# A two-layer graph network: layer 0 gathers x itself, its dense stage is woven into the end of the edge loop, and layer 1 gathers four quads ahead instead of eight

## The chip, the cores and the metric

The kernel runs on one core of one Trainium2 chip. The metric is the time of one execution on the device in microseconds (us), the median of several runs. TensorE (PE), VectorE (DVE), ScalarE (ACT), GpSimd (POOL) and SyncE (SP) each take their own instructions in order and wait for each other through semaphores.

## The reference

There are N = 6250 nodes with 128 features. 100000 drawn edges and one self loop for each node make E = 106250 edges, sorted by destination. Layer 0 is attention with one head, layer 1 one with eight heads, a learned edge term and an MLP behind it.

```
# layer 0
qk = x @ Wqk + bqk;  v = x @ Wv + bv
s[e] = clip(sum(qk[dst[e]] * qk[src[e]]) / sqrt(128), -5, 5)
attn = softmax of s over the edges of one dst
g = layer_norm(x + segment_sum(attn * v[src]) @ Wo + bo) * gamma + beta
x1 = layer_norm(x + g)
# layer 1
h = layer_norm(x1) * ln1_w
xl = h @ lin_l_w.T + lin_l_b;  xr = h @ lin_r_w.T + lin_r_b
z = leaky_relu(xl[src] + xr[dst] + edge_attr @ lin_edge_w.T, 0.2)
alpha = softmax over the edges of one dst of einsum("ehc,hc->eh", z, att)
x2 = x1 + segment_sum(xl[src] * alpha) + attn_bias
y = x2 + relu((layer_norm(x2) * ln2_w) @ fc_w.T) @ proj_w.T
out = layer_norm(x1 + y)
```

## The kernel before, in words

**Units.** The edges are cut into 832 tiles of 128 (`tiles`). Four tiles make a quad (`QT` = 4, 208 quads), four quads a group (`QUADS` = 4, 52 groups). The nodes are cut into 13 blocks of 512 (`node_groups`), each of four tiles of 128. Since edges are sorted by destination, the destinations of one tile lie in a window of 128 nodes that begins at its first one.

**Stages.** Six stages follow each other, each in a block of its own; all engines meet between two blocks. Node numbers are made ready (L110 to L143). The table `qkv_tab` is made: for each node one row of 1 KB in memory, half qk, half v (L160 to L210; PE L184, DVE L196, ACT stores at L204). Then come layer 0's edge stage (L214 to L378), its dense stage (L380 to L680), layer 1's edge stage (L683 to L1180) and the MLP (L1184 to L1490).

**Layer 0's edge stage.** For each quad, POOL issues four gathers (L260), each of which fetches the 128 rows of `qkv_tab` that belong to the sources of one tile. SP loads the four windows of destination rows (L249) and the row of edge positions `rel_bc` (L246). DVE makes from it the one-hot matrix `spread` (L334). PE multiplies it with the windows, which gives qk of each edge's destination, `q_dst` (L290), and transposes `spread` into `onehot_ps` (L296). DVE multiplies `rows` with `q_dst` and sums (`product`, L339), and clips (L375). ACT takes the exponential (L270) and scales the transposed one-hot matrix by it into `gather1` (L277). PE multiplies that with the v half of `rows` (L307) and with ones (L309) into `tile_sums`, which DVE adds to `node_sums` at the tile's first node (L348). `q_dst`, `spread` and `gather1` have two buffers each, `rows` four. The waits that tie POOL, SP and DVE to PE are these:

```
pool.wait_ge(summed, quad - QUADS + 1)            # POOL, ahead of the gathers of a quad
sp.wait_ge(q_spread, j * QUADS + q - QUADS + 1)   # SP, ahead of the windows of a quad
dve.wait_ge(summed, j * QUADS + q - 1)            # DVE, ahead of the adds of the quad two before
dve.wait_ge(q_spread, j * QUADS + q + 1)          # DVE, ahead of the scores
```

**The dense stage.** For each block of 512 nodes, PE transposes the sums of weights and spreads their inverses (L481, L490), DVE forms `mean_rows` (L561), PE multiplies by Wo (L500), DVE adds x with the bias (L569), and three layer norms follow (moments L536 and L539, roots on ACT L635, scaling on ACT L641 or DVE L589, POOL L618 to L626 for x, gamma and beta). PE transposes (L507) and multiplies with the weights of layer 1 (L516), DVE adds the biases (L582, L583), and ACT stores the tables `xl_tab` and `xr_tab`, rows of 512 bytes.

**Layer 1's edge stage.** It has the same shape: POOL gathers rows of `xl_tab` (L832), SP loads windows of `xr_tab`, edge attributes and edge positions (L812 to L816), PE makes z of a quad (L879, L883, L887; `z_ready`), ACT splits it (L843, L844), PE forms logits (L899), and once in four quads a chain of scans over DVE, PE and ACT makes the softmax. Nine quads after its z (`LAG` = 9) a quad's `message` is made on DVE (L974), multiplied on PE (L930) and added on DVE (L996). `rows` holds 16 quads (`ROWS`). POOL waits, ahead of the gathers of quad Q, for `message_made` of quad Q - 16 and for `z_ready` of quad Q - `AHEAD`, with `AHEAD` = 8.

## Time and profile before

| | us |
|---|---|
| median of 3 runs | 3092.32 (3090.11 to 3101.77) |
| profiled execution, its own time | 3122.75 |
| its span, first to last instruction | 3120.9 |
| mean granted TensorE clock in it | 0.862 of full speed |

Busy shares of the span: PE 71%, DVE 55%, ACT 21%, POOL 57%. No engine is busy all the time, so the waits say more than the shares. The profiled execution is 30.4 us (1.0%) longer than the median; sums made from its rows are made against 3122.75.

### The profile page before, as it was taken

How to read it: one execution, taken by the hardware profiler on the slowest of the kernel's cores; microseconds unless marked ns; L12 is line 12 of the kernel's file. 1: busy time of each engine (PE TensorE's matmuls, PEld its weight loads, DVE VectorE, ACT ScalarE, POOL GpSimd, SP SyncE). 2: the span in 40 equal slices, each digit the busy share in tenths (PEclk: the TensorE clock that was granted, in tenths of full speed). 3: DMA queues.
4: the chain of work that ended last, by engine and by line, in shares of the span. 5: the costliest groups of instructions: out<-in, count | busy, mean ns of one | idle time of the engine just before them, and what ended most of it. 6: DMA issues, size and time to landing. Idle time of an engine off the chain costs nothing. (4 is left out here: it accounts for less than half of the span.)

```text
span 3120.9 us, 55922 instructions
## 1 busy us (share of the span) xinstructions
PE 2211.6 (71%) x15187; PEld 1775.4 (57%) x15187; DVE 1709.5 (55%) x7262; ACT 652.8 (21%) x1876; POOL 1767.4 (57%) x1751
## 2 busy tenths in 40 slices
PE   4666666666666666656378777777777777788879
PEld 3666666666666666644255555555555555565656
DVE  4444444444444444478245555555655566565766
ACT  0222222222222222235021111111111111111123
POOL 2666666666666666644656555555555565555312
PEclk8988888888888888877688888888998999988869
DMA  6555555555555555513454444444444444444301
GB/s 212 158 150 148 152 151 150 149 151 151 149 149 151 151 151 149 139 44 88 141 163 130 121 137 133 123 130 138 137 134 120 132 139 137 137 124 130 92 15 38
DMA packets 392325, 413.24 MB, mean 132 GB/s; under 512 B 61167, under 2 KB 336367, under 8 KB 385360
## 3 DMA queue, kind: packets, MB, share of 16 engines
q1 hardware_dynamic: 304992, 233.79, 25.4%
q0 software_dynamic: 66560, 163.68, 19.3%
q10 hardware_dynamic: 20592, 13.63, 1.4%
q8 instruction: 79, 1.29, 0.2%
q14 instruction: 102, 0.84, 0.1%
HBM read 393.41 MB, written 17.47 MB: 132 GB/s over the span
## 5 line engine op out<-in xcount | busy, mean ns | idle before, releaser
L832 POOL DMA_INDIRECT rows<-xl_tab,src_cols x832 | 848.1, 1019 | 592.8 <-DVE message L974 356.4
L260 POOL DMA_INDIRECT rows<-qkv_tab,src_cols x832 | 819.7, 985 | 501.8 <-remote 250.1
L307 PE MATMUL tile_sums<-gather,rows 128*128 128x128 f32 x1664 | 401.6, 329 | 413.8 <-issue 396.8
L339 DVE CUSTOM_DVE_ANT_0 product<-rows,q_dst 128x128 f32<-128x128 f32 x832 | 233.7, 281 | 654.3 <-remote 641.5
L307 PEld LDWEIGHTS tile_sums<-gather,rows 128*128 128x128 f32 x1664 | 307.0, 230 | 460.7 <-issue 454.0
L996 DVE SCALAR_TENSOR_TENSOR node_sums<-node_sums,shrunk,tile_sums 128x128 f32 x832 | 280.7, 337 | 316.5 <-remote 294.6
L309 PE MATMUL tile_sums<-gather,ones 128*128 128x128 f32 x1664 | 380.8, 316 | 0.0
L883 PEld LDWEIGHTS z_ps<-spread,window 128*128 128x128 f32 x1664 | 253.3, 220 | 203.9 <-issue 101.8
L930 PE MATMUL tile_sums<-onehot,message 128*128 128x128 f32 x1664 | 304.3, 323 | 79.9 <-issue 72.0
L348 DVE TENSOR_TENSOR node_sums<-node_sums,tile_sums 128x256 f32 x832 | 350.8, 422 | 4.7 <-PE tile_sums L309 1.6
L930 PEld LDWEIGHTS tile_sums<-onehot,message 128*128 128x128 f32 x1664 | 245.3, 218 | 143.6 <-issue 129.9
L309 PEld LDWEIGHTS tile_sums<-gather,ones 128*128 128x128 f32 x1664 | 309.7, 232 | 0.3
L883 PE MATMUL z_ps<-spread,window 128*128 128x128 f32 x1664 | 261.7, 305 | 50.6 <-DVE spread L965 35.6
L899 PE MATMUL lg_ps<-z_act,att_pad 128*32 128x128 f32 x3328 | 206.7, 290 | 126.1 <-issue 125.1
L879 PE MATMUL z_ps<-attr,w_e 128*128 128x512 f32 x416 | 281.2, 764 | 7.6 <-issue 7.6
L290 PE MATMUL q_dst<-window,spread 128*128 128x128 f32 x1664 | 262.6, 310 | 20.8 <-issue 20.8
L290 PEld LDWEIGHTS q_dst<-window,spread 128*128 128x128 f32 x1664 | 246.0, 227 | 21.8 <-issue 21.6
L270 ACT ACTIVATE weight<-clipped 128x4 f32<-128x4 f32 x208 | 42.7, 205 | 981.7 <-DVE clipped L375 570.7
L277 ACT ACTIVATE gather<-onehot_ps,weight 128x128 f32<-128x128 f32 x832 | 237.7, 368 | 14.5 <-PE onehot_ps L296 2.8
L899 PEld LDWEIGHTS lg_ps<-z_act,att_pad 128*32 128x32 f32 x3328 | 106.1, 112 | 209.4 <-issue 205.0
L843 ACT ACTIVATE z_act<-z_ps 128x512 f32<-128x512 f32 x208 | 122.7, 590 | 425.8 <-PE z_ps L887 216.3
L984 DVE TENSOR_SCALAR onehot<-iota_row,rel_cols 128x128 f32<-128x128 f32 x832 | 179.6, 275 | 0.0
(153 smaller groups left out, 2532.8 us busy)
## 6 DMA issues: line engine op xcount, KB each, us to landing
window<-qkv_tab SPq DMA_DIRECT2D x832, 64.0 KB
attr<-in_attrT SPq DMA_DIRECT2D x52, 1024.0 KB
window<-xr_tab SPq DMA_DIRECT2D x832, 64.0 KB
rel_bc<-rel_rows SPq DMA_DIRECT2D x208, 128.0 KB
rel_bc<-rel_rows SPq DMA_DIRECT2D x52, 512.0 KB
rows<-qkv_tab,src_cols POOLq DMA_INDIRECT x832
rows<-xl_tab,src_cols POOLq DMA_INDIRECT x832
qkv_tab<-qkv ACTq DMA_DIRECT2D x13, 512.0 KB, 4.9
```

Source lines behind the costliest of these rows:

```text
L260: nc.gpsimd.indirect_dma_start(out=rows[:, q * QT + i, :], out_offset=None, in_=qkv_tab, in_offset=bass.IndirectOffsetOnAxis(ap=src_cols[: ...
L277: o = nc.scalar.mul(gather1[:, q % 2, i, :], onehot_ps[q % 2][:, i, :], weight[:, q % 2, i:i + 1])
L290: mm = nc.tensor.matmul(q_dst[q % 2][:, i, :], spread[:, q % 2, i * P:(i + 1) * P], window[:, q * QT + i, :], start=True, stop=True)
L307: nc.tensor.matmul(bank[:, i % 2, 0, :], rows[:, q * QT + i, P:], gather1[:, q % 2, i, :], start=True, stop=True)
L309: mm = nc.tensor.matmul(bank[:, i % 2, 1, :], ones[:], gather1[:, q % 2, i, :], start=True, stop=True)
L348: nc.vector.tensor_tensor(span, span, tile_sums[(q % 2) * 2 + i // 2][:, i % 2, :, :], ALU.add).then_inc(added, 1)
L832: nc.gpsimd.indirect_dma_start(out=rows[:, r, i, :], out_offset=None, in_=xl_tab, in_offset=bass.IndirectOffsetOnAxis(ap=src_cols[:, tile: ...
L879: nc.tensor.matmul(z[:], w_e[:], attr[:, s % 2, at:at + QW], start=True, stop=False)
L883: nc.tensor.matmul(z[:, i * P:(i + 1) * P], window[:, w, i, :], spread[:, Q % 2, i * P:(i + 1) * P], start=False, stop=False)
L899: mm = nc.tensor.matmul(lg_ps[s % 2][lanes, 0, :], att_pad[:, q, :], z_act[:, Q % 2, part, i * P:(i + 1) * P], start=(q == 0 and part == 0 ...
L930: mm = nc.tensor.matmul(tile_sums[Q % 2][:, i, :], message[:, Q % 2, i, :], onehot[:, Q % 2, i, :], start=True, stop=True)
L996: nc.vector.scalar_tensor_tensor(span, span, shrunk[:, Q // QUADS % 2, 1, tile % CHUNKS:tile % CHUNKS + 1], tile_sums[Q % 2][:, i, :], ALU ...
```

## The change

**One block for all of layer 0.** Stages one to four become one block without a meeting of the engines inside it, written out in full instead of in loops. Step T of it handles quad T's scores, the p of quad T + 1 and the sums of quad T - 1.

**x in place of qkv_tab.** POOL gathers rows of the input x, 512 bytes each, and waits only for the source numbers. The score is written as x[src] . p[dst] plus a constant of dst, where p = (x Wqk + bqk) Wqk^T, scaled. A table `p_tab` has 129 columns (516 bytes): p and the constant, from which the sum of the score starts. It is made in 13 blocks on PE by `make_p` (for each block four products with 129 columns and four with one row for the bias), kept and stored by ACT (`keep_p`): four blocks ahead of the first score, the other nine in steps 0 to 8. Wv and Wo are multiplied once into `w_vo` and applied to the sums.

**Halves and the one-hot matrix.** `p_dst` and `tile_sums` have one buffer for each half of a quad. PE does `spread_p` and `add_up` half by half. ACT makes the weighted one-hot matrix by itself (four Abs, an exponential, a negation, four Relu), so that the transposes of L296 go.

**The dense stage** starts at step `DENSE` = 204 and runs to step 222, one block of 512 nodes for a step, its parts 0 to 6 steps behind. Its weights are centred (`w_cen`), so that the tables need only a scale; biases go into the z of layer 1 (ACT) and the MLP; x1 is normalised in layer 1, on ACT, over quads 9 to 21. Tables have 50 tiles of 128 nodes instead of 52.

**Layer 1 and the MLP.** `AHEAD` goes from 8 to 4, `ROWS` stays 16. Semaphores of the scans are merged without a change of order. Two loads of a column and one of a bias row are added.

The core of the diff:

```diff
+    AHEAD0 = 4
+    SLOTS = 4
+    DENSE = 204
...
+                    if Q < node_groups:
+                        sp.wait_ge(p_stored[Q % 2], (Q // 2 + 1) * DMA)
+                    sp.dma_start(rel_bc[:, w, :], rel_rows[Q:Q + 1, :].to_broadcast([P, QW])).then_inc(window_in[w], DMA)
+                    for i, base in enumerate(window_bases(sp, s, Q % QUADS)):
+                        sp.dma_start(window[:, w, i, :], p_tab[bass.ds(base, P), :]).then_inc(window_in[w], DMA)
...
+                for Q in range(quads):
+                    r = Q % AHEAD0
+                    if Q >= AHEAD0:
+                        pool.wait_ge(summed, 2 * (Q - AHEAD0 + 1))
+                    for i in range(QT):
+                        tile = Q * QT + i
+                        nc.gpsimd.indirect_dma_start(
+                            out=rows[:, r, i, :], out_offset=None, in_=t["x"],
+                            in_offset=bass.IndirectOffsetOnAxis(ap=src_cols[:, tile:tile + 1], axis=0),
+                        ).then_inc(gathered[r], DMA)
...
+                def make_p(b):
+                    pe.wait_ge(x_in[b % 2], (b // 2 + 1) * DMA)
...
+                        for i in range(2):
+                            at = (k * 2 + i) * P
+                            nc.tensor.matmul(lr_ps[k][:, i, 0:P + 1], xT[:, b % 2, at:at + P], m_aug[:], start=True, stop=False)
+                            mm = nc.tensor.matmul(lr_ps[k][:, i, 0:P + 1], ones[0:1, :], m_bias[:], start=False, stop=True)
+                        mm.then_inc(p_made, 1)
...
+                def spread_p(Q, k):
...
+                    if Q:
+                        pe.wait_ge(scored, 2 * (Q - 1) + k + 1)
+                    for i in range(2):
+                        at = (2 * k + i) * P
+                        mm = nc.tensor.matmul(p_dst[k][:, i, 0:P + 1], spread[:, Q % 2, at:at + P],
+                                              window[:, Q % SLOTS, 2 * k + i, :], start=True, stop=True)
+                    mm.then_inc(p_spread, 1)
...
+                def add_up(Q, k):
+                    if k == 0:
+                        pe.wait_ge(onehot_made, Q + 1)
+                    if Q:
+                        pe.wait_ge(added, (Q - 1) * QT + 2 * k + 2)
+                    for i in range(2):
+                        nc.tensor.matmul(tile_sums[k][:, i, 0, :], rows[:, Q % AHEAD0, 2 * k + i, :],
+                                         gather1[:, Q % 2, 2 * k + i, :], start=True, stop=True)
+                        mm = nc.tensor.matmul(tile_sums[k][:, i, 1, :], ones[:], gather1[:, Q % 2, 2 * k + i, :],
+                                              start=True, stop=True)
+                    mm.then_inc(summed, 1)
+
...
+                    for i in range(n):
+                        at = b * QW + i * P
+                        mm = nc.tensor.matmul(o_ps[:, i, :], node_sums[:, 0, at:at + P], w_vo[:], start=True, stop=True)
+                    mm.then_inc(projected, 1)
...
+                    for i in range(block_tiles(b)):
+                        mm = nc.tensor.matmul(lr_ps[i // 2][:, i % 2, :], hT[:, i, :], w_cen[:], start=True, stop=True)
...
+                pe.wait_ge(w_loaded, 6 * DMA)
...
+                pe.wait_ge(m_kept, 4)
+                for b in range(QUADS):
+                    make_p(b)
+                spread_p(0, 0)
+                spread_p(0, 1)
+                for T in range(steps):
+                    for k in range(2):
+                        if T + 1 < quads:
+                            spread_p(T + 1, k)
+                        if 0 <= T - 1 < quads:
+                            add_up(T - 1, k)
+                    if T + QUADS < node_groups:
+                        make_p(T + QUADS)
+                    b = T - DENSE
+                    if b == 0:
+                        pe.wait_ge(w_scaled, 1)
+                        pe.wait_ge(ident_made, 2)
+                        pe.wait_ge(p_kept, 2 * node_groups)
+                        nc.tensor.matmul(lr_ps[0][:, 0, :], ident_c[:], w_lr[:], start=True, stop=True).then_inc(w_centred, 1)
...
+                    for i in range(QT):
+                        tile = Q * QT + i
+                        o = nc.scalar.activation(apart[:, i, :], iota_row[:], ACT.Abs, bias=rel_cols[:, tile:tile + 1],
+                                                 scale=-1.0)
+                    o.then_inc(apart_made, 1)
...
+                    for i in range(QT):
+                        o = nc.scalar.activation(gather1[:, Q % 2, i, :], apart[:, i, :], ACT.Relu,
+                                                 bias=weight[:, Q % 2, i:i + 1], scale=minus[:, Q % 2, i:i + 1])
+                    o.then_inc(onehot_made, 1)
...
+                    for i in range(n):
+                        o = nc.scalar.mul(xlr[:, b % 2, i, :], lr_ps[i // 2][:, i % 2, :], rstd[:, 1, b % 2, i:i + 1])
+                    o.then_inc(lr_kept, 1)
...
-    AHEAD = 8
-    SLOTS = 4
-    quads = tiles // QT
+    AHEAD = 4
```

PE's instructions for one quad in the middle of layer 0's edge stage, before (the names are those of the sections above):

```order
L290 MATMUL q_dst<-window,spread 128x128 x4
L296 MATMUL onehot_ps<-ident,spread 128x128 x4
L307 MATMUL tile_sums<-gather,rows 128x128
L309 MATMUL tile_sums<-gather,ones 128x128
L307 MATMUL tile_sums<-gather,rows 128x128
L309 MATMUL tile_sums<-gather,ones 128x128
L307 MATMUL tile_sums<-gather,rows 128x128
L309 MATMUL tile_sums<-gather,ones 128x128
L307 MATMUL tile_sums<-gather,rows 128x128
L309 MATMUL tile_sums<-gather,ones 128x128
```

and of the change, one quad with what each piece waits for:

```order
L309 MATMUL p_dst<-window,spread 128x129 [waits scored,window_in1,spread_made]
L309 MATMUL p_dst<-window,spread 128x129
L319 MATMUL tile_sums<-gather,rows 128x128 [waits added,onehot_made]
L321 MATMUL tile_sums<-gather,ones 128x128
L319 MATMUL tile_sums<-gather,rows 128x128
L321 MATMUL tile_sums<-gather,ones 128x128
L309 MATMUL p_dst<-window,spread 128x129 [waits scored]
L309 MATMUL p_dst<-window,spread 128x129
L319 MATMUL tile_sums<-gather,rows 128x128 [waits added]
L321 MATMUL tile_sums<-gather,ones 128x128
```

What was one piece of eight matmuls (four of `q_dst`, four transposes) and one of eight (the sums) is now two halves, each of two for `p_dst` and four for the sums, and each half waits for DVE's scores and adds of the same half.

DVE in the dense stage, one block of 512 nodes, before:

```order
L561 TENSOR_TENSOR mean_rows<-node_sums,inv_ps 128x512
L569 TENSOR_TENSOR h<-o_ps,x_o 128x512
L536 BN_STATS stats<-h 128x6 x4
L539 BN_AGGR mv<-stats 128x2 x4
L547 RECIPROCAL rstd<-std 128x4
L548 SCALAR_TENSOR_TENSOR shift<-mv,rstd 128x4
L555 RECIPROCAL inv<-w_ps 128x32
L587 RECIPROCAL rstd<-std 128x4
L589 TENSOR_SCALAR x<-h,mv,rstd 128x128 x4
L582 TENSOR_TENSOR xlr<-lr_ps,b_lr 128x512
L583 TENSOR_TENSOR xlr<-lr_ps,b_lr 128x512
L536 BN_STATS stats<-x 128x6 x4
```

and one block of the change, in a step past the last quad:

```order
L613 TENSOR_TENSOR x_nm<-x_nm,b_vo 128x512
L588 RECIPROCAL rstd<-std 128x4
L590 SCALAR_TENSOR_TENSOR shift<-mv,rstd 128x4
L608 RECIPROCAL rstd<-std 128x4
L561 RECIPROCAL share<-t_ps 128x4
L567 SCALAR_TENSOR_TENSOR h<-o_ps,share,x_nm 128x128 x4
L596 BN_STATS stats<-x 128x6 x4
L600 BN_AGGR mv<-stats 128x2 x4
L574 BN_STATS stats<-h 128x6 x4
L580 BN_AGGR mv<-stats 128x2 x4
```

One of the three rounds of moments, the scaling of L589, `mean_rows` and the two bias additions over 512 columns are gone; four operations over 128 columns (L567) and one over 512 (L613) are there instead.

POOL in layer 1's edge stage, its first gathers, before:

```order
L832 DMA rows<-xl_tab,src_cols 128x128 x32
L832 DMA rows<-xl_tab,src_cols 128x128 [waits z_ready]
L832 DMA rows<-xl_tab,src_cols 128x128 x3
```

and of the change:

```order
L834 DMA rows<-xl_tab,src_cols 128x128 x16
L834 DMA rows<-xl_tab,src_cols 128x128 [waits z_ready]
L834 DMA rows<-xl_tab,src_cols 128x128 x3
```

The first run without a wait shrinks from 32 gathers to 16.

## Rows read from the trace of the kernel before

**Rows 1.** By stretch: length, busy PE, PEld, DVE, ACT, POOL, PE clock, DMA share, GB/s.

```profile
0.00:70.00 70.00, 27.72 (x113) 23.18 (x114) 32.75 (x38) 1.28 (x1) 12.95 (x19) 0.86 0.70 224
70.00:1335.00 1265.00, 848.11 (x5817) 800.61 (x5815) 593.11 (x2910) 280.43 (x1040) 807.24 (x820) 0.87 0.54 149
1335.00:1489.00 154.00, 82.95 (x364) 65.52 (x364) 117.67 (x496) 66.81 (x170) 65.56 (x52) 0.76 0.25 70
1489.00:1547.00 58.00, 15.21 (x76) 9.28 (x77) 15.84 (x27) 2.40 (x5) 40.50 (x43) 0.56 0.56 158
1547.00:2996.00 1449.00, 1129.24 (x8201) 797.80 (x8195) 867.56 (x3428) 256.61 (x570) 808.41 (x792) 0.87 0.43 128
2996.00:3120.90 124.90, 108.37 (x624) 79.02 (x624) 82.59 (x365) 45.23 (x92) 32.72 (x26) 0.92 0.12 33
```

**Rows 2.** Timeline of POOL in layer 0's edge stage: start, length, engine, line.

```profile
707.64 0.95 POOL L260 DMA_INDIRECT rows<-qkv_tab,src_cols  x1 [1.16 <-remote]
...
711.54 0.96 POOL L260 DMA_INDIRECT rows<-qkv_tab,src_cols  x1 [0.30 <-issue]
713.75 0.95 POOL L260 DMA_INDIRECT rows<-qkv_tab,src_cols  x1 [1.26 <-remote]
```

**Rows 3.** Timeline of PE and DVE in the same stretch.

```profile
709.99 0.60 PE L296 MATMUL onehot_ps<-ident,spread 128*128 128x128 f32 x4
713.23 0.39 PE L309 MATMUL tile_sums<-gather,ones 128*128 128x128 f32 x2
713.71 0.29 DVE L339 CUSTOM_DVE_ANT_0 product<-rows,q_dst 128x128 f32<-128x128 f32 x1 [3.30 <-remote]
```

**Rows 4.** Groups by line: busy, mean ns, idle before and what ended it.

```profile
L832 POOL DMA_INDIRECT rows<-xl_tab,src_cols x832 | 848.1, 1019 | 592.8 <-DVE message L974 356.4 <-issue 225.6 <-remote 8.7
L260 POOL DMA_INDIRECT rows<-qkv_tab,src_cols x832 | 819.7, 985 | 501.8 <-remote 250.1 <-issue 193.0 <-POOLq L162 52.8
L339 DVE CUSTOM_DVE_ANT_0 product<-rows,q_dst 128x128 f32<-128x128 f32 x832 | 233.7, 281 | 654.3 <-remote 641.5 <-issue 7.6 <-PE q_dst L290 5.0
L277 ACT ACTIVATE gather<-onehot_ps,weight 128x128 f32<-128x128 f32 x832 | 237.7, 368 | 14.5 <-PE onehot_ps L296 2.8 <-remote 1.1
```

**Rows 5.** Timeline of POOL in layer 1's edge stage, and its last gather.

```profile
2201.32 1.03 POOL L832 DMA_INDIRECT rows<-xl_tab,src_cols  x1 [2.00 <-DVE message L974]
...
2216.02 1.75 POOL L832 DMA_INDIRECT rows<-xl_tab,src_cols  x1 [4.83 <-DVE message L974]
...
2228.81 1.03 POOL L832 DMA_INDIRECT rows<-xl_tab,src_cols  x1 [2.02 <-DVE message L974]
...
2929.84 0.95 POOL L832 DMA_INDIRECT rows<-xl_tab,src_cols  x1 [0.30 <-issue]
```

**Rows 6.** Busy time from the last gather to the MLP.

```profile
2930.80:2996.00 65.20, 47.53 (x339) 38.07 (x331) 55.85 (x218) 9.07 (x21) 0.00 (x0) 0.71 0.05 11
```

**Rows 7.** Timeline of layer 0's start.

```profile
53.93 1.11 POOL L260 DMA_INDIRECT rows<-qkv_tab,src_cols  x1 [52.77 <-POOLq L162]
...
67.93 2.08 PE L290 MATMUL q_dst<-window,spread 128*128 128x128 f32 x8 [20.41 <-issue]
...
70.05 0.29 DVE L339 CUSTOM_DVE_ANT_0 product<-rows,q_dst 128x128 f32<-128x128 f32 x1 [1.78 <-issue]
...
73.95 1.14 ACT L277 ACTIVATE gather<-onehot_ps,weight 128x128 f32<-128x128 f32 x4 [2.55 <-PE onehot_ps L296]
```

**Rows 8.** DMA issues: size, and median us from issue to landing.

```profile
qkv_tab<-qkv ACTq DMA_DIRECT2D x13, 512.0 KB, 4.9
```

**Rows 9.** Timeline of DVE in the dense stage.

```profile
1412.41 1.11 DVE L589 TENSOR_SCALAR x<-h,mv,rstd 128x128 f32<-128x128 f32 x4
1413.44 0.68 DVE L582 TENSOR_TENSOR xlr<-lr_ps,b_lr 128x512 f32<-128x512 f32 x1
```

**Rows 10.** Timeline of POOL: layer 1's first gather.

```profile
1490.01 0.99 POOL L832 DMA_INDIRECT rows<-xl_tab,src_cols  x1 [0.17 <-issue]
```

**Rows 11.** DMA queue of SP in layer 0's edge stage: packets, MB, share.

```profile
q1 hardware_dynamic: 146880, 80.28, 23.7%
```

## What the change should do to the time: the prediction

> **What bounds the kernel now.** I read the stretches first. Layer 0's edge stage takes 1265 us for 208 quads, 6.08 us each, and PE is busy there for 848 us, POOL 807, DVE 593, ACT 280: nobody is full [rows 1]. Layer 1's takes from the first gather at 1490.0 to the MLP at 2996 [rows 1, 10]. So I went on to POOL's own timeline. A run of four gathers begins at 707.64 and at 713.75, 6.11 apart; the fourth begins 3.90 after the first and lasts 0.96, so a run is 4.86, and 1.26 of idle time follows [rows 2]. The groups put 250.1 us of POOL's waiting down to 200 such gaps, and all but 13 of the 654 us of waiting ahead of DVE's products to a "remote" event [rows 4]. What is that event? At 713.71, 3.30 us idle, DVE's next product starts. It waits for `q_spread`, for sums of two quads ago and for its rows. PE finished its transposes, which come behind `q_dst`, at 710.6, over three us before [rows 3]. Yet DVE starts within 0.04 us of POOL's next run, about 1.1 us after the fourth gather has ended. I read this so: what PE signals while POOL is in a run reaches the others only some 1.1 us after the run. A quad therefore costs one run and one such gap, whatever PE and DVE do in between.
>
> Layer 1 is the same with longer runs. Runs begin at 2201.32, 2216.02 and 2228.81: eight gathers each, 13.7 us for two quads, 6.87 a quad, and the gaps are 2.0 and 4.8 us, ended by `message` [rows 5]. There, 356.4 us go to the wait for `message` [rows 4]. That the engines could go faster shows behind the last gather (2930.8): with POOL silent, the rest takes 65.2 us [rows 6]. The last gathered quad is 7 to 8 ahead of its z, which is 9 ahead of its message, so this is some 16 quads at 4.1 us.
>
> **The change, part by part.**
>
> *Layer 0's quad: 6.08, then 6.05, worth nothing.* POOL still issues four gathers, each 128 rows; their 0.985 us was that of issuing [rows 4], and I keep it although rows halve. It waits for the sums of the quad four before, as it did. A step of PE loses the four transposes (0.60) [rows 3] and DVE nothing. ACT gains four Abs and a negation: with four Relu that is eight times 0.368 and two small ones, about 3.3 us of 6.1 [rows 4], hidden. `p_dst` is single now, so each half of `spread_p(T+1)` waits for the scores of T in the same half and gives its result in the same run: one passage from PE to DVE for a quad, as before. Bounds: gain 0 to 1.0 us a quad (the gap gone), loss to 1.1.
>
> *The start: -28.* The first product comes at 70.05, behind the whole table and the first gathers at 53.93 [rows 7]. Now POOL begins at about 5 and only four blocks of p are ahead. Loads 8, folding the weights 5, `make_p` four times 2.1 to 4.2 (eight products each, by the 2.08 us that eight passes took at the start, and half that at full clock) [rows 7], a store of 4.9 [rows 8], four windows and the spread 6: 32 to 41. If PE's results are held back under the first run of 16 gathers (the one-hot matrices reached ACT only at 73.95, 2.55 us of waiting, while a run went on) [rows 7], 50. I take 42.
>
> *Nine blocks of p inside steps 0 to 8: +12.* PE had 848/208 = 4.1 us a step [rows 1], less 0.6, plus 2.1 to 4.2 for `make_p`: up to 7.7 against 6.08. Bounds 0 and +20.
>
> *Dense stage: -53.* From 1335 to the first gather at 1490 it took 155 us; DVE was busy for 117.67 of it, 9.05 a block of 512 nodes [rows 1, 10]. Of this go L589 (1.11), two additions over 512 columns for `xlr`, `mean_rows` and `h` (four times 0.6 from start to start of such a pair), a round of moments (1.2) and a reciprocal (0.3); four operations as in L589 (1.11) and one over 512 columns (0.6) come [rows 9]. That leaves 5.75; less a little because the last four steps hold only moments, 5.4. Steps 210 to 222 are 13 times 5.4 = 70. In steps 204 to 207 dense work lies beside a quad: 9 instead of 6.08, +12. Steps 208 and 209, sums and dense, 18. With 2 for the meeting of the engines: 102 against 155. The load of weights and x behind the edge stage is covered by the edge loop. Bounds: 90 to 135.
>
> *Layer 1: -160.* Before, from the first gather to the MLP: 1506. After: POOL issues 16 gathers (20 us, at 1.26), waits some 8 for the first z, then gathers 204 quads. With `AHEAD` = 4, z of quad Q-4 is followed by message Q-13, while the wait wants Q-16: three quads of slack where there was none. So POOL waits for z alone and its runs are of four, as in layer 0: 6.07. PE is busy for 1129 us here, 5.3 a quad [rows 1], and ACT has biases and, for 13 quads, four more operations; I take 6.2. 204 times 6.2 = 1265. The rest behind the last gather is 13 quads instead of 16, at 4.1: 53. Sum 20 + 8 + 1265 + 53 = 1346. Bounds: 5.9 a quad (some waits end inside a gap) and 6.87 (nothing gained).
>
> *MLP: 0.* One addition on POOL at its start, ahead of a stage in which PE is busy for 108 of 125 us [rows 1].
>
> Sum: -28 + 12 - 53 - 160 = -229 against 3122.75, 2894 for a profiled execution. The one of before stood 30 above the median, so 2864 as a median; I say 2865.
>
> **A rule against the change.** The windows of layer 0 move from rows of 512 bytes to rows of 516. SP's queue held 23.7% of the DMA engines' time in this stage [rows 11], all engines 54% [rows 1]. The Trainium skill says (DMA: Bandwidth & Descriptors, How a descriptor splits into AXI transactions) that a descriptor which does not start at a multiple of 256 bytes costs additional transactions; by it a window would cost up to twice as much. By the rows, twice 23.7% is still under the whole with the gathers halved, and windows are asked for three quads ahead, so neither gives another time for a quad.
>
> **The rivals.**
> - *Layer 1 keeps its 6.87* because the softmax chain, not the message wait, sets it: 204 times 0.67 = +137, so about 3000. For it: DVE and PE pass results several times in each group of four quads. Against it: the 4.1 us without gathers. Chance 0.15.
> - *Layer 0 speeds up too*, since half the bytes end the 1.1 us gap: 5.03 to 5.5 a quad, -120 to -215, so 2650 to 2745. Against it: layer 1's rows are already of 512 bytes and its gaps are no shorter [rows 5]. Chance 0.08.
> - *Slower*: the halves need two passages from PE in one quad. If `spread_p` of the second half falls behind POOL's gap each time, a step waits for a second run or part of one, up to 12 us a step. The change is slower than before once a step costs 1.09 us more (227/208), 7.2; at 7.5 it is 3165. For it: `add_up` waits for DVE's adds of the same half, which wait for their scores. Chance 0.06.
> - *The new start and the dense stage bring nothing* (the tail of steps 208 to 222 is held up by results of PE or POOL): +60, 2925. Chance 0.1.
>
> **How the numbers follow.** The forecast above has 0.61. Its own range is 2800 to 2930. The range for 8 in 10 takes in the fourth rival and most of the first: 2765 to 2990. 0.5% is 15 us, about what a measurement of this kernel can tell. All cases but the third are faster, together 0.94; of these I put 0.03 to within 0.5%, where the first and the fourth rival come together with a loss of their own. Faster by more: 0.91; within: 0.03; slower: 0.06.
>
> **What would show it.** In the profile after, POOL's runs in layer 0 are still of four, 6.0 to 6.1 apart, with a gap of about 1.1; the first product comes near 42; the first gather of layer 1 stands near 1420; in layer 1 the wait for `message` is gone from POOL's groups and runs of four stand 6.1 to 6.3 apart. The prediction is wrong if the step of layer 0 leaves 6.1 in either direction, or if layer 1 stays at 6.9.

## The result, and the profile after

| | before | after |
|---|---|---|
| median, us | 3093.3 (3090.11 to 3101.77, 4 runs) | 2996.8 (2986.7 to 2999.9, 4 runs) |
| ratio | | 0.968, 95% interval 0.965 to 0.971 |
| span of the profiled execution, us | 3120.9 | 2997.0 |
| mean granted clock | 0.862 | 0.823 |

The change makes the kernel 3.2% faster, 97 us. I had forecast 228 us, and the result lies 7 us above the range. By its own time the profiled execution is 124 us shorter (2998.8 against 3122.75), where the sum had 229: 105 us to account for. The two profiles do not stand alike to their medians: the one before lies 30 us above its own, the one after 2. So some 27 of the 124 us are no gain of the change, and the median misses its forecast by 132 us (2997 against 2865). The parts below set a forecast worked from a slower execution against a quicker one, and so show 27 us too little of the miss.

Busy time by stretch in the changed kernel (length, then busy PE, PEld, DVE, ACT and POOL, PE clock, DMA share, GB/s; compare [rows 1]):

```profile
0.00:44.00 44.00, 28.05 (x84) 19.73 (x85) 7.69 (x21) 5.22 (x13) 16.35 (x22) 1.00 0.54 149
44.00:183.00 139.00, 107.19 (x480) 90.33 (x480) 55.46 (x219) 54.60 (x162) 46.17 (x49) 0.80 0.42 104
183.00:1320.00 1137.00, 756.54 (x4575) 708.51 (x4574) 611.56 (x2666) 634.52 (x1909) 729.20 (x764) 0.80 0.46 112
1320.00:1486.90 166.90, 108.18 (x434) 92.31 (x432) 72.12 (x363) 71.20 (x175) 52.73 (x46) 0.64 0.20 55
1486.90:2871.00 1384.10, 1120.74 (x8271) 796.50 (x8271) 884.90 (x3458) 314.55 (x623) 849.54 (x832) 0.85 0.47 141
2871.00:2997.00 126.00, 107.73 (x624) 78.81 (x624) 82.68 (x365) 46.16 (x92) 33.37 (x27) 0.92 0.12 33
```

The first row ends with the first product (44.0; 42 was forecast), the second with the gathers of quad 16, the third with those of quad 207. The fourth is the end of the edge stage with the dense stage, up to layer 1's first gather. The cuts come from POOL's timeline:

```profile
182.71 0.95 POOL L268 DMA_INDIRECT rows<-in_x,src_cols  x1 [1.29 <-PE tile_sums L321]
...
1324.31 0.95 POOL L268 DMA_INDIRECT rows<-in_x,src_cols  x1 [0.30 <-issue]
...
1486.92 0.99 POOL L834 DMA_INDIRECT rows<-xl_tab,src_cols  x1 [0.17 <-issue]
...
1583.31 0.96 POOL L834 DMA_INDIRECT rows<-xl_tab,src_cols  x1 [1.82 <-remote]
...
2815.68 0.96 POOL L834 DMA_INDIRECT rows<-xl_tab,src_cols  x1 [0.30 <-issue]
```

Quads 16 to 207 of layer 0 are 191.75 quads up to their last gather, so one takes 1141.6 / 191.75 = 5.95 us; in layer 1 it is 1232.4 / 191.75 = 6.43. Counted the same way, before had 6.11 and 7.00. Against the forecast's own dates the 105 us are made up so:

| part | forecast | measured | miss |
|---|---|---|---|
| first product | 42 | 44.0 | +2 |
| from it to the gathers of quad 16 (13 steps) | 13 x 6.05 + 12 = 91 | 138.7 | +48 |
| quads 16 to 207 (191 steps) | 191 x 6.05 = 1156 | 1137.8 | -18 |
| from the gathers of quad 207 to layer 1's first | 132 | 166.4 | +34 |
| layer 1, first gather to the MLP | 1346 | 1384 | +38 |
| MLP | 125 | 126 | +1 |

(132 is what the forecast's 1421 for the first gather leaves behind 42 + 91 + 1156.)

### The profile page after: what moved, and what is told of

Same layout as the page of the kernel before. It is cut to its first block and busy times, and to the rows that moved or that the text cites. A ratio compares the mean times of both kernels' runs of the same rounds, so it can differ in the third digit from the quotient of the medians.

```text
span 2997.0 us, 52661 instructions
## 1 busy us (share of the span) xinstructions
PE 2228.4 (74%) x14461; PEld 1786.2 (60%) x14461; DVE 1714.4 (57%) x7092; ACT 1126.3 (38%) x2973; POOL 1727.4 (58%) x1739
## 3 DMA queue, kind: packets, MB, share of 16 engines
q8 instruction: 118, 1.93, 0.3%
## 5 line engine op out<-in xcount | busy, mean ns | idle before, releaser
L834 POOL DMA_INDIRECT rows<-xl_tab,src_cols x832 | 849.5, 1021 | 480.3 <-issue 230.6
L268 POOL DMA_INDIRECT rows<-in_x,src_cols x832 | 795.0, 956 | 529.1 <-issue 208.6
L319 PE MATMUL tile_sums<-gather,rows 128*128 128x128 f32 x1664 | 431.0, 350 | 287.3 <-DVE node_sums L549 213.1
L319 PEld LDWEIGHTS tile_sums<-gather,rows 128*128 128x128 f32 x1664 | 334.3, 249 | 325.2 <-issue 233.8
L309 PE MATMUL p_dst<-window,spread 128*128 128x129 f32 x1664 | 336.4, 337 | 141.8 <-issue 87.6
L309 PEld LDWEIGHTS p_dst<-window,spread 128*128 128x128 f32 x1664 | 290.4, 246 | 158.2 <-issue 147.3
L537 DVE CUSTOM_DVE_ANT_0 product<-rows,p_dst 128x128 f32<-128x128 f32 x832 | 258.3, 348 | 188.8 <-remote 127.6
L432 ACT ACTIVATE gather<-apart,weight,minus 128x128 f32<-128x128 bf16 x832 | 342.6, 482 | 7.1 <-issue 0.2
L321 PEld LDWEIGHTS tile_sums<-gather,ones 128*128 128x128 f32 x1664 | 333.6, 249 | 0.0
L845 ACT ACTIVATE z_act<-z_ps,z_bias 128x512 f32<-128x512 f32 x208 | 141.6, 681 | 474.8 <-remote 283.1
L418 ACT ACTIVATE apart<-iota_row,rel_cols 128x128 bf16<-128x128 f32 x832 | 265.7, 390 | 10.5 <-issue 3.8
```

The costliest lines, as they stand in the source:

```text
L268: nc.gpsimd.indirect_dma_start(out=rows[:, r, i, :], out_offset=None, in_=t["x"], in_offset=bass.IndirectOffsetOnAxis(ap=src_cols[:, tile: ...
L309: mm = nc.tensor.matmul(p_dst[k][:, i, 0:P + 1], spread[:, Q % 2, at:at + P], window[:, Q % SLOTS, 2 * k + i, :], start=True, stop=True)
L319: nc.tensor.matmul(tile_sums[k][:, i, 0, :], rows[:, Q % AHEAD0, 2 * k + i, :], gather1[:, Q % 2, 2 * k + i, :], start=True, stop=True)
L321: mm = nc.tensor.matmul(tile_sums[k][:, i, 1, :], ones[:], gather1[:, Q % 2, 2 * k + i, :], start=True, stop=True)
L432: o = nc.scalar.activation(gather1[:, Q % 2, i, :], apart[:, i, :], ACT.Relu, bias=weight[:, Q % 2, i:i + 1], scale=minus[:, Q % 2, i:i + 1])
L834: nc.gpsimd.indirect_dma_start(out=rows[:, r, i, :], out_offset=None, in_=xl_tab, in_offset=bass.IndirectOffsetOnAxis(ap=src_cols[:, tile: ...
```

## The experiments

The runs stand in groups that shared a chip, and each ratio is to the kernel before on that chip. Its median was 3102 us beside e1 to e4 (chip number 10 in the record), 3125 beside e5, e6, e7 and c1_three_orders (15), 3123 beside e9, e10, c2 and c1_again (4), 3090 beside after_again, c1_fourth and e11_again (11), and 2564 beside c1_third, e11_alpha_late and e12 (4 again); the last group has a section of its own below. The last column is the time of one quad from quad 16 on, counted as above. It depends on the group: the same layer 0 takes 5.95 to 5.96 us a quad where before took 3090 to 3102, and 6.02 to 6.04 where it took 3123 to 3125. So quads are compared inside a group.

| run | ratio to before | 95% interval | first gather of layer 1 | quad, layer 0 / 1 |
|---|---|---|---|---|
| changed kernel | 0.968 | 0.965 to 0.971 | 1486.9 | 5.95 / 6.43 |
| after_again | 0.967 | 0.963 to 0.971 | 1477.5 | 5.96 / 6.42 |
| e1_weigh_first | 0.953 | 0.950 to 0.956 | 1441.3 | 5.96 / 6.43 |
| e2_hT_first | 0.955 | 0.952 to 0.958 | 1448.9 | 5.96 / 6.45 |
| e3_project_first | 0.960 | 0.957 to 0.963 | 1453.2 | 5.96 / 6.45 |
| e4_before_ahead4 | 0.961 | 0.958 to 0.964 | 1473.5 | 6.01 / 6.44 |
| e5_three_gathers | 0.887 | 0.885 to 0.889 | 1235.4 | 4.73 / 6.55 |
| e6_ahead8 | 1.001 | 1.000 to 1.002 | 1495.0 | 6.03 / 7.03 |
| e7_ahead3 | 0.973 | 0.970 to 0.975 | 1492.1 | 6.03 / 6.58 |
| c1_three_orders | 0.945 | 0.944 to 0.947 | 1408.7 | 6.04 / 6.58 |
| e9_l1_three_gathers | 0.897 | 0.894 to 0.899 | 1498.0 | 6.02 / 5.44 |
| e10_l1_edge_quarter | 0.965 | 0.964 to 0.967 | 1494.9 | 6.03 / 6.48 |
| c2_dense202 | 0.943 | 0.940 to 0.946 | 1399.7 | 6.04 / 6.51 |
| c1_again | 0.941 | 0.939 to 0.944 | 1404.6 | 6.03 / 6.50 |
| c1_fourth | 0.938 | 0.934 to 0.943 | 1400.0 | 5.96 / 6.41 |
| e11_again | 0.941 | 0.937 to 0.945 | 1389.3 | 5.95 / 6.40 |

### The first steps: a ring through ACT's order (e1)

Steps 0 to 8 took 10 to 14 us each. What held them is called a ring here: a closed chain of waits, in which each engine waits for the one before it and the first for the last, so that their times add up. The timeline of the changed kernel in one of them, PE and ACT:

```profile
91.48 0.48 PE L298 MATMUL lr_ps<-m_bias,ones 1*128 1x129 f32 x2
92.00 0.37 ACT L409 COPY p_rows<-lr_ps 128x258 f32<-128x258 f32 x1 [1.24 <-PE lr_ps L298]
92.40 0.40 ACTq L411 DMA_DIRECT2D p_tab<-p_rows  x1
92.84 0.52 ACTq L402 DMA_DIRECT2D xT<-in_xT  x1
93.41 0.20 ACT L424 ACTIVATE weight<-clipped 128x4 f32<-128x4 f32 x1 [1.04 <-issue]
93.88 1.65 ACT L432 ACTIVATE gather<-apart,weight,minus 128x128 f32<-128x128 bf16 x4
95.58 0.80 PE L319 MATMUL tile_sums<-gather,rows 128*128 128x128 f32 x2 [2.98 <-ACT gather L432]
```

ACT's weights stand behind `keep_p`, which waits for PE's last product of `make_p`. PE's sums of the next step wait for the weights (2.98 us), and the next `make_p` stands behind the sums. So PE's work and ACT's, 3.6 us from the copy to the sums, follow each other instead of lying side by side. DVE had clipped long before.

```diff
                 for T in range(steps):
                     if T < quads:
                         measure(T)
                     if T + QUADS < node_groups:
+                        weigh(T)
                         keep_p(T + QUADS)
...
-                    if T < quads:
+                    if T + QUADS >= node_groups and T < quads:
                         weigh(T)
```

> The changed kernel, with one edit: in steps 0 to 8 ACT does weigh(T) ahead of keep_p(T + 4), not behind it. In the changed kernel's trace these steps take 11 to 14 us each. Theory A: they are a ring of waits, PE make_p, then ACT keep_p and two transfer issues, then ACT's weights, then PE's sums, then make_p again. Then the steps fall to 8 to 9.5 us and the kernel gains 20 to 35 us against the changed one (a ratio to before of about 0.960). Theory B: PE is simply full there (at its lower clock) with the eight more products, or the steps wait for p_tab's windows. Then nothing changes (within 5 us).

Measured: ratio 0.953, layer 1's first gather at 1441.3, 45.6 us sooner. Quad 16 was gathered at 137.3 and not at 182.7; other executions with the old order had it between 170.9 and 182.7, so that 34 to 45 us are the edit's. The forecast of 133 for this point is nearly reached. POOL's timeline at the same place:

```profile
85.99 0.95 POOL L268 DMA_INDIRECT rows<-in_x,src_cols  x1 [2.92 <-PE tile_sums L321]
...
92.05 0.95 POOL L268 DMA_INDIRECT rows<-in_x,src_cols  x1 [1.33 <-PE tile_sums L321]
...
99.65 0.95 POOL L268 DMA_INDIRECT rows<-in_x,src_cols  x1 [2.87 <-PE tile_sums L321]
```

Steps of 6.1 and 7.6 us: theory A, with shorter steps than the 8 to 9.5 us and a larger gain than the 20 to 35 us that it had.

### The dense stage: two more rings (e2, e3)

In steps behind the last quad DVE, whose work I had costed, waits. The changed kernel, one of these steps:

```profile
1411.15 3.19 PE L354 MATMUL lr_ps<-w_cen,hT 128*128 128x256 f32 x8
...
1414.18 0.60 PE L346 MATMUL t_ps<-ident,x 128*128 128x128 f32 x4
1414.38 1.57 ACT L469 ACTIVATE xlr<-lr_ps,rstd 128x256 f32<-128x256 f32 x4 [4.72 <-PE lr_ps L354]
...
1417.01 0.59 ACT L460 COPY hT<-t_ps 128x512 f32<-128x512 f32 x1 [1.06 <-issue]
...
1417.74 1.83 PE L335 MATMUL t_ps<-ones,node_sums 1*128 1x1 f32 x8 [2.96 <-ACT hT L460]
...
1419.51 2.08 PE L339 MATMUL o_ps<-w_vo,node_sums 128*128 128x128 f32 x8
...
1421.38 1.06 PE L354 MATMUL lr_ps<-w_cen,hT 128*128 128x256 f32 x2
1421.62 0.18 DVE L561 RECIPROCAL share<-t_ps 128x4 f32<-128x4 f32 x1 [3.33 <-PE o_ps L339]
```

From 1411.15 to 1421.38 the ring goes round once: the tables on PE, the turning, ACT's scaling and two transfer issues, hT on ACT, and only then may PE project the next block, for the sums of weights land in `t_ps`, which hT is read from. 10.2 us, of which DVE is busy for 4.6 (for 6.0 in the step from 1380.0). PE waits in it, and the granted clock is 0.64 over this stretch.

```diff
+                    if 0 <= b - 5 < blocks:
+                        keep_hT(b - 5)
                     if 0 <= b - 6 < blocks:
                         keep_tables(b - 6)
-                    if 0 <= b - 5 < blocks:
-                        keep_hT(b - 5)
```

> The changed kernel, with one edit: in the dense stage ACT does keep_hT(b - 5) ahead of keep_tables(b - 6). In the changed kernel's trace the steps behind the last quad take 10.2 us each, DVE being busy for 6 of them. Theory A: they are a ring over PE and ACT (project, tables, turn_y on PE, then xlr, two issues and hT on ACT, then project of the next block, which needs t_ps). Then seven steps lose 2.3 us each, together 16 us, and the last steps, which wait for the scaled tables instead, lose nothing. Theory B: DVE's work or the wait for the roots on ACT sets the step. Then nothing changes.

Measured: ratio 0.955. From the last gather of layer 0 to the first of layer 1 it took 129.7 us instead of 162.6, 33 less, twice what A had. The steps fell from 10.2 to 5.6 to 7.6 us. Two of them in POOL's timeline of e2_hT_first:

```profile
1386.24 1.26 POOL L282 TENSOR_TENSOR u<-u,gamma 128x512 f32<-128x512 f32 x1 [1.78 <-ACT u L451]
...
1392.30 1.27 POOL L282 TENSOR_TENSOR u<-u,gamma 128x512 f32<-128x512 f32 x1 [1.78 <-ACT u L451]
```

I had taken 2.3 us a step off the ring and forgotten that the next table then lies beside ACT's scaling as well, 4.1 us in all. So the ring was the limit. Without it a step takes about what DVE's work does, as I had forecast for all of them: of the 6.06 us between the two rows DVE is busy for 5.9, a little over the forecast 5.4. (The same operations took 4.6 us in the step of 10.2; here L613 takes 1.32 us and not 0.66, and L590 0.91 and not 0.16.)

Beside the last quads, from step 204 on, another ring of 10 to 11 us runs: DVE waits 3.6 and 5.3 us for `project` (L339), its next scores and adds stand behind, and PE's sums wait for these (4.74 us). PE and DVE in the timeline of the changed kernel:

```profile
1349.99 0.77 PE L319 MATMUL tile_sums<-gather,rows 128*128 128x128 f32 x2 [4.74 <-DVE node_sums L549]
...
1357.58 0.18 DVE L561 RECIPROCAL share<-t_ps 128x4 f32<-128x4 f32 x1 [5.34 <-PE o_ps L339]
```

```diff
                 for T in range(steps):
+                    b = T - DENSE
+                    if 0 <= b < blocks:
+                        project(b)
                     for k in range(2):
...
-                    if 0 <= b < blocks:
-                        project(b)
```

> The changed kernel, with one edit: PE does project(b) at the beginning of a step, ahead of spread_p and add_up, not at its end. In the changed kernel's trace steps 204 to 209 take 10.4 us each. Theory A: they are a ring too: DVE waits 3.6 to 5.3 us for project, behind it stand the next step's scores and adds, and PE waits 4.7 us for those adds before its sums. Then these six steps fall to 7.5 to 9 us, a gain of 8 to 18 us in all. Theory B: the sum of ACT's work with its changes of function table sets the step. Then nothing changes.

Measured: ratio 0.960. A step beside a quad fell to 7.76 us (L282 starts at 1327.65 and at 1335.41 in POOL's timeline). Counted from the last gather, the fifth L282 starts after 34.5 us and not after 52.2, 18 us sooner, and the part from the last gather to layer 1 fell to 139.3 us, 23 less. Theory A, a little above its bounds.

> The changed kernel with the three edits of order together (weights ahead of keep_p in steps 0 to 8, keep_hT ahead of keep_tables, project at the beginning of a step). Apart they brought layer 1's first gather from 1486.9 to 1440.4, 1448.0 and 1452.2 us. Theory A: they mend three rings in different steps, so they add up but for the 12 us by which the first steps differ from run to run: first gather at 1365 to 1385, ratio about 0.93. Theory B: they work on the same wait. Then together they bring little more than the best alone, 1440.

Measured: ratio 0.945, and 0.941 and 0.938 in two repeats; the first gather at 1408.7, 1404.6 and 1400.0. On one chip the changed kernel took 2991.5 us and this one 2904.7, 87 less. Alone, the three ratios lie 0.015, 0.013 and 0.008 below the changed kernel's, 111 us together. So they add up for the most part, as A had it, but not to its 1365 to 1385: e2 and e3 together bring the part behind the last gather to 113 to 120 us in the three runs, where the old order took 159 to 164 on the same chips. That is 39 to 51 less, group by group, and not 56. The forecast date of the first gather, 1421, is passed. This is the fastest order that I found, 6% below before.

One more edit moves the dense stage two steps ahead (`DENSE = 202` in place of 204).

> The changed kernel with the three edits of order and DENSE = 202, so that two more steps of the dense stage lie beside quads. With the three edits a step beside a quad took 7.7 us, one behind the last quad 6.06. Theory A: two steps less behind the last quad, and two beside one, 1.7 us longer each, gain 8 to 10 us on the three edits alone (ratio about 0.942). Theory B: ACT, which must wait for POOL to finish its gathers before it may norm the third block, stalls the edge loop; then nothing is gained, or up to 10 us lost.

> The changed kernel with the three edits of order once more, beside the others on this chip: ratio 0.945, layer 1's first gather near 1400 us.

Measured: 0.943 against 0.941 on the same chip, intervals overlap. No gain, as B had it; whether by the stall it names was not looked into.

### What a quad costs: POOL's run and its gap (e5, e9)

In e5 the fourth tile is not gathered and its rows are read from the third's:

```diff
-                    for i in range(QT):
+                    for i in range(3):
                         tile = Q * QT + i
                         nc.gpsimd.indirect_dma_start(
```

> The changed kernel with a quarter of layer 0's gathers left out: POOL gathers three tiles of a quad instead of four, and DVE and PE read the third tile's rows where they read the fourth's. All other work of a quad is the same. In the changed kernel a quad takes 5.96 us in the middle of the edge stage. Theory A: a quad costs POOL's run and the gap behind it, nothing else. Then it falls to 4.6 to 4.9 us (one gather of 1.26 us less), 220 to 260 us over 192 quads, ratio about 0.89. Theory B: the ring over PE, DVE and ACT, whose handing on is slow, sets the quad. Then it stays at 5.8 to 6.0.

Measured: a quad in layer 0 falls from 6.03 (e6 and e7, the same chip) to 4.73, 1.30 us for one gather of 1.26. POOL's timeline in e5 shows a run of three and the gap of [rows 2]:

```profile
616.04 0.95 POOL L268 DMA_INDIRECT rows<-in_x,src_cols  x1 [2.31 <-PE tile_sums L321]
617.29 0.95 POOL L268 DMA_INDIRECT rows<-in_x,src_cols  x1 [0.30 <-issue]
618.55 0.95 POOL L268 DMA_INDIRECT rows<-in_x,src_cols  x1 [0.30 <-issue]
620.66 0.95 POOL L268 DMA_INDIRECT rows<-in_x,src_cols  x1 [1.15 <-PE tile_sums L321]
```

B is out: the ring over PE, DVE and ACT can go at 4.7. The same edit in layer 1:

> The changed kernel with a quarter of layer 1's gathers left out: POOL gathers three tiles of a quad, the fourth tile's rows are set to zero once. All other work is the same. In the changed kernel a quad takes 6.45 us there, POOL idles 1.96 us behind a run on average, and PE is busy for 5.3 us a quad. Theory A: POOL's run and the gap behind it set the quad. Then it falls by 0.9 to 1.26 us, to 5.2 to 5.5, 190 to 250 us in all (ratio near 0.90). Theory B: PE's own work with its waits sets it. Then it falls by less than 0.4 us.

Measured: 5.44 against 6.50 (c1_again, same layer 1, same chip), 1.06 us less, as A had it. But PE was quicker too: over these quads the mean granted clock was 0.96 and PE busy for 897 us, against 0.85 and 1034 us in c1_again. How much of the gain that is, this run does not separate.

### Layer 1: the distance, and what is left (e4, e6, e7, e10, e11, e12)

```diff
-    AHEAD = 8
+    AHEAD = 4
```

> The kernel before, with the change's one number in layer 1: AHEAD = 4 instead of 8. In the changed kernel layer 1 takes 1385 us from its first gather to the MLP against 1506 before. Theory A: all of this is the shorter distance, which takes the wait for message out of POOL's way. Then this kernel is 115 to 125 us faster than before (ratio about 0.961), and faster than the changed one. Theory B: the merged semaphores and the biases moved to ACT have a part in it. Then the gain here differs from 121 us by more than 15.

Measured: 0.961, 122 us, with nothing else of the change. This number alone gives more than the whole change did: with the rest of it, as it was ordered, the kernel is about 0.7% slower. The reverse:

> The changed kernel with AHEAD = 8 in layer 1, as before. Theory A: the distance alone gives layer 1's gain. Then layer 1 takes 1500 to 1510 us from the first gather to the MLP, and the kernel is 110 to 125 us slower than the changed one, about level with the kernel before (ratio 1.00 to 1.01). Theory B: the merged semaphores and the moved biases give a part; then it stays below 1490 us.

Measured: 1.001, 7.03 us a quad, layer 1 at 1510 us. By the ratios that is 0.033 or 103 us slower than the changed kernel, a little less than A's 110 to 125, and it puts the cost of the rest at 0.1%. The wait for `message` is back, 364.8 us in POOL's group, as in [rows 4]; in the changed kernel it has left the head of that group (POOL's gathers of layer 1 in the groups by line):

```profile
L834 POOL DMA_INDIRECT rows<-xl_tab,src_cols x832 | 849.5, 1021 | 480.3 <-issue 230.6 <-remote 167.6 <-PE z_ps L901 67.9
```

> The changed kernel with AHEAD = 3 in layer 1. With 4 a quad takes 6.45 us there and still about half of the gathers come in runs of eight, not of four, with the longer gaps. Theory A: the run's length sets the cost of a quad. Then shorter runs give 6.1 to 6.3 us a quad, a gain of 30 to 70 us on the changed kernel (ratio 0.945 to 0.96). Theory B: the exchange of results between PE, DVE and ACT sets 6.45, and less distance makes z wait for the rows. Then nothing changes or a quad gets longer.

Measured: 0.973, a quad 6.58 where 4 had 6.58 on the same chip. Theory B: less than 4 buys nothing.

Of the 480.3 us of idle time some 211 are the 0.3 between two gathers of a run. The other 269 lie in the 140 gaps of POOL's timeline, 1.9 us each (1.75 behind a run of four, 2.1 behind one of eight). Before, 371 of the 592.8 us [rows 4] lay in 104 gaps, 3.6 each. In layer 0 the gap is 1.2 [rows 2], which I had carried over. The runs are not all of four either, as I had forecast: 73 are, 47 are of eight and 7 of twelve. PE's z comes late now and then, as PE and POOL in the timeline of the changed kernel show:

```profile
2108.49 1.93 PE L893 MATMUL z_ps<-attr,w_e 128*128 128x512 f32 x2
...
2110.21 1.91 PE L897 MATMUL z_ps<-spread,window 128*128 128x128 f32 x8
...
2113.73 0.96 POOL L834 DMA_INDIRECT rows<-xl_tab,src_cols  x1 [2.33 <-PE z_ps L901]
```

POOL's last gather of the run before ended at 2111.4 and z was done at 2113.0, at half clock (1.93 us for what took 1.02 to 1.12 in the next two steps). Two tests of why. The first takes work off PE:

```diff
-                    nc.tensor.matmul(z[:], w_e[:], attr[:, s % 2, at:at + QW], start=True, stop=False)
+                    nc.tensor.matmul(z[:, 0:P], w_e[:], attr[:, s % 2, at:at + P], start=True, stop=False)
```

> The changed kernel with three quarters of the edge term left out: PE multiplies only the first 128 of a quad's 512 columns of edge attributes with their weights, 1.0 us less of PE's work in a quad; the loads stay. Theory A: a result of PE that misses POOL's gap waits for the next one, and PE, at 5.3 us busy of 6.45, often misses it. Then a quad falls from 6.45 to 6.0 to 6.2 us, the 6.0 of layer 0, a gain of 50 to 90 us. Theory B: the chain of scans on DVE and ACT makes the longer gaps. Then a quad stays above 6.35.

Measured: 6.48, against 6.50 (c1_again) and 6.51 (c2) on the same chip. But the test does not decide. From quad 16 on the mean granted clock was 0.81, where it is 0.85 in c1_again, and PE was still busy for 974 us of 1243, against 1034 of 1246, though it did only a quarter of this product's columns. The stretches, of c1_again and of e10_l1_edge_quarter:

```profile
1501.22:2747.39 1246.17, 1033.76 (x7647) 741.47 (x7646) 804.60 (x3182) 286.94 (x567) 785.54 (x768) 0.85 0.46 143
1591.34:2834.45 1243.11, 974.12 (x7601) 757.25 (x7602) 796.57 (x3159) 284.88 (x565) 778.61 (x767) 0.81 0.46 143
```

The second moves PE's wait for alpha behind z:

```diff
-                    if Q % QUADS == 1 and 0 <= s - 1 < groups:
-                        turn_alpha(s - 1)
                     if Q + 1 < quads:
                         make_z(Q + 1)
+                    if Q % QUADS == 1 and 0 <= s - 1 < groups:
+                        turn_alpha(s - 1)
```

> The three edits of order, and in layer 1 PE does turn_alpha behind make_z(Q + 1), not ahead of it, once in four quads. In a stretch of the changed kernel PE waits 1.0 us for alpha, then makes z at half its clock, and z is done 1.6 us behind POOL's last gather. Theory A: these waits make z late and the gap long; then a quad loses 0.1 to 0.3 us (one z in four comes 1 to 2 us sooner), 20 to 60 us in all. Theory B: z is late because PE's own work between two gaps (logits, sums, z: 5.9 us at full clock) hardly fits, wherever alpha stands; then nothing changes, within 5 us.

> The changed kernel with the three edits of order, as the base of the next two: ratio 0.940 to 0.946, a quad of layer 1 6.5 us on this chip.

> As e11, and sum_ends and spread_shares too stand behind make_z(Q + 1). Theory A: 30 to 80 us less than the base. Theory B: no gain. Theory C: results of the chain of scans miss POOL's gap and reach DVE and ACT one run of gathers later; then message comes late, and the kernel is 20 to 100 us slower than the base.

Measured in the group where before took 2564 us: base 0.979 (0.977 to 0.980), e11 0.974 (0.972 to 0.976), e12 0.979 (0.977 to 0.981). With the gaps there:

> turn_alpha behind make_z(Q + 1). Without the gaps 12 us less than its base, as measured. With them: theory A, z is late because PE waits for alpha ahead of it: 20 to 60 us less than the base. Theory B: within 5 us of the base.

> The three edits of order, as the base on this chip: ratio 0.941 to 0.945 with the gaps, 0.979 without.

Measured: e11 0.941 and base 0.938, overlapping: no gain there. So waits for alpha are not what makes z late. That leaves PE's own work between two gaps, B of e11, as the likely cause; this is argued, not shown.

### A group of runs in which the gap is missing (c1_third)

In one group the kernel before took 2564 us (2560 to 2566, 7 runs), 17% less than in all others, and the kernel with the three orders 2510. No trace of before was taken there. The timeline of POOL in layer 0 in c1_third, to be held against [rows 2]:

```profile
600.24 0.95 POOL L268 DMA_INDIRECT rows<-in_x,src_cols  x1 [0.30 <-issue]
601.50 0.96 POOL L268 DMA_INDIRECT rows<-in_x,src_cols  x1 [0.30 <-issue]
602.76 0.95 POOL L268 DMA_INDIRECT rows<-in_x,src_cols  x1 [0.30 <-issue]
604.02 0.95 POOL L268 DMA_INDIRECT rows<-in_x,src_cols  x1 [0.30 <-issue]
605.28 0.95 POOL L268 DMA_INDIRECT rows<-in_x,src_cols  x1 [0.30 <-issue]
```

and DVE and PE of the same kernel at the same time:

```profile
603.71 0.35 DVE L539 CUSTOM_DVE_ANT_0 product<-rows,p_dst 128x128 f32<-128x128 f32 x1 [2.67 <-DMA rows<-in_x,src_cols]
...
604.49 0.68 PE L309 MATMUL p_dst<-window,spread 128*128 128x129 f32 x4 [2.71 <-DVE scores L539]
```

A gather takes the same 0.95 us and the same 0.30 stand between two. But there is no gap behind four of them. POOL's waits are met while it still issues, a quad costs 5.07 us, four times 1.26, and in layer 1, where a gather takes 1.03 us on average, 5.35. DVE's scores and PE's products start in the middle of a run; what DVE waits for is rows that have not landed. So the gap is not a cost of the program alone. It was there in every trace of the other groups. Nor is it shown to be a property of the chip: the record gives this group the chip number 4, and the same number to the group of e9, e10, c2 and c1_again, eight minutes earlier, where the gaps were there, before took 3123 us and the very same kernel (c1_again) 2935. What makes the difference, these runs do not show.

> The changed kernel itself. Where the gaps behind POOL's runs are there (the kernel before near 3100 us): ratio 0.965 to 0.971, as before. Where they are missing (the kernel before near 2564 us) and theory A holds, that nearly all of layer 1's gain is fewer and shorter gaps: layer 1 gains under 20 us, the start gains, the first steps and the dense stage lose as they did, so the ratio is 0.985 to 1.005.

Measured: this group had the gaps; ratio 0.967. What the change alone is worth without gaps stays open. Since the three orders made it faster elsewhere, c1_third's 0.979 is probably its lower bound, which is argued only.

## Why the prediction was wrong

- **The start, -28:** right (44.0 against 42). The feared holding back of PE's results under the first 16 gathers is in the rows (ACT's copy of p at 26.92 waited 7.3 us) and cost little.
- **The parts are 27 us too kind:** the profile of before lay 30 us above its median, that of the change 2. To take the 30 off at the end was right, but in the table each part of the forecast still holds its share of them. It shows in the quads of both layers, below.
- **Nine blocks of p, "+12, bounds 0 and +20": the step that failed worst.** Measured +60 over 13 steps. I had added PE's busy times and compared them with the period. I named neither what stands behind `keep_p` on ACT nor who waits for that; the weights stand there, and PE's sums wait for them. e1 gives back 34 to 45 us.
- **The dense stage, -53, bounds 90 to 135: failed.** It came to 166 from the gathers of quad 207, forecast 132 (136 by the forecast's own count, where it had 102). The sum counted DVE, as the engine that had been busy before. The changed order makes a ring over PE and ACT of 10.2 us (e2) and one over PE and DVE of 10 to 11 (e3). With both mended the part from the last gather to layer 1 takes 113 to 120 us instead of 159 to 164.
- **A quad of layer 0, nothing gained:** mechanism right where the gap exists (e5), and the size nearly too. The measured 5.95 leaves 6.1, which I had named as a sign of being wrong, and the sum came out 18 us better. But where before took 3123 to 3125 us, as in its profile, the changed layer 0 takes 6.02 to 6.04 a quad, forecast 6.05, and layer 0 of before itself takes 6.01 in e4, in the group of 3102 us, against 6.11 in the profile. So most of the 18 us are the quicker group and not the change. A smaller thing that I had not foreseen: 51 of the 154 runs are now of eight, with one gap of 2.1 us for two quads.
- **Layer 1, -160:** mechanism right, shown alone (122 us from the one number in e4, 103 by the ratio of e6). Mis-sized term: 6.43 us a quad, not 6.2, 192 quads times 0.23 = 44 us; where before took 3123 to 3125 us, as in its profile, it is 6.50 to 6.58, which makes the miss 58 to 73 us. I had taken the idle time behind a run over from layer 0, 1.2 us; it is 1.9, and some of it is a late z. The 13 quads behind the last gather took 54.4 us, forecast 53.
- **The rule on 516-byte rows (the Trainium skill, DMA: Bandwidth & Descriptors, How a descriptor splits into AXI transactions):** by the rows, SP's queue had 23.8% of the engines' time in quads 16 to 207 before and 27.9% now, 279 us for 136800 packets and 318 us for 138906: 12 to 13% more for a packet, not twice. "Up to twice" was also worked out wrongly: a row of 516 bytes touches three stretches of 256 bytes where an aligned one of 512 touches two, half more. No quad got longer, as said.
- **The rivals:** the fourth (start and dense stage bring nothing, 2925) was near the right place and had too small a price: the two terms it takes away, 28 and 53, make 81 and not 60, the start did bring its part, and the loss beside it lay in steps 0 to 8, which no rival named. That the steps' halves need two passages from PE did not happen.

## What to carry to other kernels

When work is woven into another stage's steps, list for every engine what stands behind each new wait, and follow that until the ring closes; comparing busy sums with the period missed 82 us here, and the cure was only the order of a few calls. A number that removes a wait (how far ahead to gather) is worth testing alone: it gave 122 us, more than the change around it. And measure a kernel more than once, at other times and on other chips, before a gap in its timeline is taken for a law, and compare stages only between runs in which the kernel before took the same time.

## What the runs showed of the hardware

- POOL's runs of gathers are followed by a gap, 1.2 us behind four in layer 0, at whose end the waiting engines go on together. In one group of runs there was none, and the same kernel before was 17% faster; the chip number was that of a group with gaps. A gather is issued in 0.95 + 0.30 us in both cases, and for rows of 512 bytes and of 1 KB alike.
- Less work on PE did not make a quad shorter: with three quarters of one product left out, the mean granted clock was 0.81 over the same quads and not 0.85, PE was busy for 974 us and not 1034, and a quad took 6.48 us and not 6.50. Without the gaps the clock stood at 0.92 there (c1_third).
